# A fused post-norm transformer kernel on one core: ACT instead of SP begins the DMAs of the max rows in layer-0 attention

## What is computed

```python
qkv = x @ Wqkv                      # 16 heads of 8
q, k = _apply_rope(q, cos, sin), _apply_rope(k, cos, sin)
att = jnp.einsum('bhqd,bhkd->bhqk', q, k) * scale
att = jnp.where(causal, att, -jnp.inf)
att = jax.nn.softmax(att, axis=-1)
out = jnp.einsum('bhqk,bhkd->bhqd', att, v)
return out.transpose(0, 2, 1, 3).reshape(B, T, C) @ Wo + bo
```

## Time and profile before

| | |
|---|---|
| median of 3 runs | 938.85 us (935.68 to 939.76) |
| the profiled execution | 941.87 us, its span 940.1 us |
| mean granted clock of TensorE | 0.885 of full speed |
| PE matmul busy | 707.0 us, 75% of the span |
| PE weight load busy | 403.2 us, 43% |
| DVE busy | 552.9 us, 59% |
| ACT busy | 472.9 us, 50% |
| POOL busy | 494.9 us, 53% |
| DMAs of the hardware queue of SP | 79.63 MB |

### The profile page before, as it was taken

The page is one execution under the profiler, slowest core; times in us unless marked ns, Lnnn a source line. Parts: engine busy times, 40 slices in busy tenths (PEclk is TensorE's granted clock), DMA queues, the critical chain, the costliest instruction groups (busy, mean ns, idle before and its releaser), DMA issues. The chain is left out here.

```text
span 940.1 us, 17909 instructions
## 1 busy us (share of the span) xinstructions
PE 707.0 (75%) x6254; PEld 403.2 (43%) x6254; DVE 552.9 (59%) x1408; ACT 472.9 (50%) x708; POOL 494.9 (53%) x652
## 2 busy tenths in 40 slices
PE   6837999999569999999958839999995423777800
PEld 2413555555333344444424316777773212454500
DVE  6857888888258877777776732344346464121116
ACT  4433767777456666666636745666662500222202
POOL 5833767767344454544524655666664301588741
PEclk9975999999889999999988978999997755799955
DMA  4773463431000000000004679999971510244353
GB/s 143 234 216 59 116 182 98 113 90 27 2 1 1 0 1 0 2 0 1 0 1 134 218 223 177 199 196 187 176 110 52 152 32 4 64 94 95 61 96 105
DMA packets 134982, 86.06 MB, mean 92 GB/s; under 512 B 10864, under 2 KB 131440, under 8 KB 134768
## 3 DMA queue, kind: packets, MB, share of 16 engines
q1 hardware_dynamic: 128112, 79.63, 37.3%
q0 software_dynamic: 5632, 4.33, 3.4%
q10 hardware_dynamic: 1152, 0.98, 0.3%
HBM read 55.02 MB, written 29.49 MB: 90 GB/s over the span
## 5 line engine op out<-in xcount | busy, mean ns | idle before, releaser
L772 POOL TENSOR_TENSOR m_prod<-m_upc,m_gatec 128x512 f32<-128x512 f32 x64 | 99.6, 1556 | 110.7 <-DVE m_upc L602 110.7
L2143 ACT ACTIVATE a_prob<-a_ps_pair 128x1024 f32<-128x1024 f32 x96 | 94.8, 1022 | 59.4 <-PE a_ps_pair L1995 38.3
L2155 POOL TENSOR_SCALAR_AFFINE_SELECT a_prob<-a_prob 128x512 f32<-128x512 f32 (+1 forms) x96 | 75.5, 787 | 58.5 <-ACT a_prob L2143 58.5
L1827 ACT ACTIVATE a_prob<-a_ps_pair 128x1024 f32<-128x1024 f32 x96 | 96.3, 1023 | 16.3 <-PE a_ps_pair L1631 13.6
L1868 POOL TENSOR_SCALAR_AFFINE_SELECT a_prob<-a_prob 128x512 f32<-128x512 f32 (+1 forms) x96 | 75.5, 787 | 45.1 <-ACT a_prob L1827 44.3
L1769 DVE TENSOR_REDUCE a_mx<-a_ps_pair 128x4 f32<-128x1024 f32 x64 | 77.7, 1219 | 22.1 <-PE a_ps_pair L1672 20.5
L707 ACT ACTIVATE m_gate<-m_ps_g,bgu 128x512 f32<-128x512 f32 x64 | 43.9, 686 | 55.0 <-PE m_ps_g L453 54.9
L476 PE MATMUL m_ps_d<-m_act,wd 128*128 128x512 f32 x128 | 65.6, 594 | 2.3 <-DVE m_act L612 2.3
L1341 POOL DMA_INDIRECT m_y<-normed,idx x32 | 31.1, 970 | 68.5 <-POOLq L80 59.1
L453 PE MATMUL m_ps_g<-m_x1T,wgu 128*128 128x512 f32 x128 | 66.1, 598 | 0.0
L455 PE MATMUL m_ps_u<-m_x1T,wgu 128*128 128x512 f32 x128 | 65.4, 592 | 0.0
(11 more groups left out here) (277 smaller groups left out, 1658.0 us busy)
## 6 DMA issues: line engine op xcount, KB each, us to landing
qst<-scratch_q SPq DMA_DIRECT2D x64, 128.0 KB, 4.2
kst<-scratch_k SPq DMA_DIRECT2D x64, 128.0 KB, 4.2
scratch_q<-p_parts SPq DMA_DIRECT2D x16, 384.0 KB, 2.6
scratch_k<-p_parts SPq DMA_DIRECT2D x16, 384.0 KB, 2.6
qst<-scratch_q SPq DMA_DIRECT2D x32, 192.0 KB, 4.8
kst<-scratch_k SPq DMA_DIRECT2D x32, 192.0 KB, 5.4
w<-in_w SPq DMA_DIRECT2D x8, 578.0 KB, 4.0
scratch_q<-parts SPq DMA_DIRECT2D x16, 256.0 KB, 2.5
```

Source lines behind the costliest of these rows:

```text
L772: nc.gpsimd.tensor_tensor(prod[:, n % 2, :], upc[:, n % 2, :], gatec[:, n % 2, :], ALU.mult).then_inc(s_pr, 1)
L1827: nc.scalar.activation(prob[:, r % 6, :], pair[(0, 2, 1)[j]][:, :], ACT.Exp, scale=scale, bias=0.0).then_inc(s_e, 1)
L2143: nc.scalar.activation(prob[:, r % 6, :], pair[r % 2][:, :], ACT.Square, scale=scale, bias=1.0).then_inc(s_e, 1)
L2155: nc.gpsimd.affine_select(out=blk, in_=blk, compare_op=ALU.is_ge, fill=0.0, base=0, pattern=[[0, n], [1, P]], channel_multiplier=-1).then_ ...
```

## The change

`max_rows` moves from SP's program to ACT's. In ACT's pass u it stands behind `copy_max(u + 2)` and `copy_att` and ahead of `exp(u, 2)`. The wait for `s_mTc` (the copy is done), the two DMAs and their semaphore are the same.

```diff
--- before.py
+++ after.py
@@ -1575,22 +1575,12 @@
         with nc.Block() as block:
             @block.sync
             def _(sp):
-                def max_rows(w):
-
-                    sp.wait_ge(s_mTc, w + 1)
-                    for m in range(2):
-                        r0 = 64 * m + max_row
-                        sp.dma_start(qst[r0:r0 + 3, w % BUFS, :, :].rearrange("p h (x q) -> p (h x) q", q=P),
-                                     mT[24 * m:24 * m + 24, w % 2, :]).then_inc(s_mrow[w % 2], 16)
-
                 def load_x(i):
                     part = slice(NTILE // 4 * i, NTILE // 4 * (i + 1))
                     sp.dma_start(xn[:, part, :], io["x"].rearrange("(t p) c -> p t c", p=P)[:, part, :]).then_inc(s_xn, 16)
 
                 later = list(consts["later"].items())
                 for u in range(1 - LEAD, NU):
-                    if u + 2 < NU:
-                        max_rows(u + 2)
                     if u == -1:
                         load_x(0)
                         load_stacks(sp, 3, stacks, scratch, s_st[3])
@@ -1830,6 +1820,14 @@
                     act.wait_ge(s_mT, w + 1)
                     nc.scalar.activation(mT[:, w % 2, :], ps_y[0:48, 0:64].bitcast(BF16), ACT.Copy).then_inc(s_mTc, 1)
 
+                def max_rows(w):
+
+                    act.wait_ge(s_mTc, w + 1)
+                    for m in range(2):
+                        r0 = 64 * m + max_row
+                        act.dma_start(qst[r0:r0 + 3, w % BUFS, :, :].rearrange("p h (x q) -> p (h x) q", q=P),
+                                      mT[24 * m:24 * m + 24, w % 2, :]).then_inc(s_mrow[w % 2], 16)
+
                 def copy_out(n):
                     act.wait_ge(s_pv, n + 1)
                     after(act, s_tp, n - 1)
@@ -1852,6 +1850,8 @@
                         copy_max(u + 2)
                     if b is not None:
                         copy_att(b)
+                    if 0 <= u + 2 < NU:
+                        max_rows(u + 2)
                     if 0 <= u < NU:
                         exp(u, 2)
```

## The result

The changed kernel took 990.31 us in the median (989.58 to 991.96), the kernel before 939.31 us beside it: a ratio of 1.0549, 95% interval 1.0513 to 1.0586. It is 51 us slower. The forecast was 989 us, with a range of 960 to 1019.

The account below looks back on a forecast made before the run. PE and the chain ACT, POOL, PE, ACT were taken to bound each attention unit together. Profiled: 941.87 + 40.5 (insert) + 3 (contention) + 10 (clock) - 3.5 (late rows) = 991.9 us; median 989 us, range 960 to 1019.

Parts of the forecast that it names:

- The chain: Layer-0 attention, ACT, POOL, PE, ACT: closes once a unit; anything between `copy_max` and third exponential lengthens the unit fully.
- The size of the insert: ACT, `copy_max` to third exponential: 1.84 us without `copy_att` (+1.51), 1.87 with it (+1.17); +40.5 us in all.
- The overlap with `copy_att`: On ACT, issues begin 0.37 us after `copy_max` began, while `copy_att` runs: +1.17 us a unit instead of +1.54.
- Nothing takes it up.: After the third exponential, no later slack absorbs the delay: each unit keeps its 4.98 or 5.15 us plus the insert.
- The sign that was named: In the changed profile, third exponentials of successive attention units should start 6.5 and 6.3 us apart.
- Contention: ACT's issues running beside SP's DMA issues take longer: +3 us taken, between nothing and 7.5 us.
- SP's relief: Max rows leave SP's queue, so PE's two long waits for late rows vanish: -3.5 us.
- a queue without stack loads ahead: Max rows issued on ACT go out as soon as copied, with no stack loads before them, so should be in time.
- rival A: Issues cost ACT next to nothing as arithmetic runs on; only SP is relieved: at most 933 us, chance 0.03.
- The clock: PE's new waits in attention units drop its clock to 1.2 GHz for a few us: ten times 1.0 us, +10 us.
- The ten: Number of places where PE's clock falls, at 1.0 us each, taken between none and 30.

## Why the prediction was right

**The chain.** That the third exponential stands on a chain that closes once a unit was right, and is shown, not only argued: with the same issues behind it the change costs 2 us, and another load of like length ahead of it costs 49.

**The size of the insert.** Forecast 1.84 and 1.87 us from `copy_max` to the exponential, measured 1.85 and 1.92. The wait for ACT's own copy, alone, cost 0.06 us at most. The price of an issue on SP (0.72) carried over to ACT (0.73); ACT's own shorter rows at the start, of other transfers, would have misled. The overlap with `copy_att`, read from one pair of rows, was there in every unit.

**"Nothing takes it up."** Wrong by a little. In the unit that follows a `copy_att`, PE and not the chain had been last: 4.65 us lay between the third exponential and `copy_max`, and 4.44 lie there now (111.18 to 115.62). So the beat grew by 1.31 and not by 1.51, in some 15 units 3 us in all. The run with one issue shows the same 0.2 us. The sign that was named, beats of 6.5 and 6.3 us, did not come: they are 6.29 and 7.39, the first shorter by this slack, the second longer by the clock.

**Contention.** Forecast +3 us, measured next to none: of the 64 issues 44 overlap one of SP's in time, and none of these took more than 0.76 us; the one of 1.36 us is the very first and stands beside none.

**SP's relief.** The waits for the rows vanished, as forecast (-3.5 us). Their cause was half right. The short wait was, by the trace of that one execution, that of rows held back behind SP's stack loads. The long one, 2.25 of the 3.5 us, was not: its rows were issued in time, right behind 1.5 MB of weights; splitting the stack loads left it, moving the weights removed it. So the prediction's "a queue without stack loads ahead" does not explain why no row was late in the changed kernel. There ACT issued the rows of unit 8 at 129.61, half a microsecond after the first weight load, as in the version with each issue under an exponential; but PE needed them only at 138.47, 7.4 us after the issues had ended, and in that version they took 6.4. The longer units hid the delay. (The 6.0 us of the earlier trace rows add PE's matmuls, 2.6, and its weight loads, 3.4, which waited at the same time for the same rows; rival A's 933 us would have been 935 or 936.)

**The clock.** Forecast ten falls at 1.0 us, 10 us. The size of one was right, their number too low: in every pair of units the clock fell once, 12 long units of 1.0 us each, and three at the start were long too. Against the run with PE's gap filled the beats add up to 14 us more, though the matmuls added there lengthened its other units by some 2 us. That run shows that this is the clock, as it gives 11 us back in the median. The ten was a pick between 0 and 30 with nothing to tell them apart, so that it came near is luck.

The sum: the profiled execution grew by 50.1 us, and 50.0 were forecast. The two steps that were too high (3 us of slack, 3 us of contention) stand against the clock that was too low (4 us or more) and the 1 us ahead of the attention, which is in no term of it. That these cancel to within 0.1 us is luck; that the place has a price, some 37 us where 40.5 were forecast, was foreseen by its mechanism. Rival A (the issues are free) was wrong at this place, but it is what happens at another: under an exponential they are free.

## What to carry to other kernels

A DMA issue holds its engine's queue for its whole time, here 0.73 us, while arithmetic that was started before it runs on; so put it right behind a long instruction, and never between two steps of the chain that closes a loop. Busy share does not tell whether there is room: ACT was idle a quarter of the time, and a load in the wrong place still cost nearly its full length. What such a load leaves as a gap on PE can cost once more through the clock. A small transfer that something waits for can come late when it is begun beside a large one, here 1.5 MB, whatever queue either is on; it needs room between issue and use, or the large one another place.

## What was not expected of the hardware

An issue and an activation on ACT overlap fully: 1.50 us of issues and 1.43 us of arithmetic took 1.85 us with the copy ahead of them, as the issues did alone. And regular short waits of PE let the granted clock fall again and again. In the changed kernel the waits for the third exponential were 1.1 us on average and 1.4 at the most; with the unused activation in their place none was over 1.0 us, and the clock still fell in eleven pairs of units, where single waits of 1.19 and 1.13 us had left it up. How long a wait is does not tell alone whether the clock falls.
